# The expert stage of a gated cross-attention and mixture-of-experts block turned round: weights stationary, each expert's tokens as one moving pass of 336 slots

## What is computed

```python
x = x + tanh(g_xattn) * attention(layernorm(x), ctx)     # 120 context rows a sequence, softmax, one head of 256
x = x + tanh(g_ffn)   * experts(layernorm(x))

# experts: H = 256, I = 704, E = 8; every token goes to one expert
e = argmax(router_w @ h)                                 # top 1 of 8
y = down_w[e] @ (silu(gate_w[e] @ h) * (up_w[e] @ h))
```

## Time and profile before

| what | value |
|---|---|
| median of 3 runs (lowest, highest) | 221.98 us (221.41, 222.62) |
| span of the profiled execution | 218.9 us |
| TensorE, matmul busy | 199.7 us, 91% |
| TensorE, weight load busy | 170.9 us, 78% |
| GpSimd (POOL) busy | 136.1 us, 62% |
| VectorE (DVE) busy | 130.8 us, 60% |
| ScalarE (ACT) busy | 109.8 us, 50% |
| HBM read, written | 24.85 MB, 4.72 MB; 135 GB/s over the span |

### The profile page before, as it was taken

How to read it: one execution, slowest core, us unless ns; L and a number is a source line. 1 busy time by engine, 2 the same in 40 slices (tenths; PEclk the granted TensorE clock), 3 DMA queues, 4 the chain that set the end, 5 groups by cost and what they waited for, 6 DMA issues and landing times.

```text
span 218.9 us, 4538 instructions
## 1 busy us (share of the span) xinstructions
PE 199.7 (91%) x1200; PEld 170.9 (78%) x1200; DVE 130.8 (60%) x430; ACT 109.8 (50%) x223; POOL 136.1 (62%) x138
## 2 busy tenths in 40 slices
PE   7899999997665789999999999999999999999960
PEld 3667998985564678888888888888888888888850
DVE  2886899867699125537555537564636565645650
ACT  1478777664500534495269485369475444422410
POOL 3004099495473897339966998987998985212111
PEclk9999999999787589999999999999999999999996
DMA  6999315928600319621581085194003012011000
GB/s 208 340 394 378 135 49 163 368 73 291 217 0 0 99 25 358 211 68 38 189 313 32 0 311 189 34 383 126 1 8 92 0 51 68 9 49 51 5 28 20
DMA packets 11845, 29.43 MB, mean 134 GB/s; under 512 B 1986, under 2 KB 8517, under 8 KB 10790
## 3 DMA queue, kind: packets, MB, share of 16 engines
q1 hardware_dynamic: 6320, 20.20, 25.9%
q0 software_dynamic: 2064, 5.12, 7.8%
q10 hardware_dynamic: 3430, 3.74, 5.1%
HBM read 24.85 MB, written 4.72 MB: 135 GB/s over the span
## 4 chain that ended last, share of the span: by engine, by line
PE 83%; DVE 6%; ACT 3%; DMA 3%; issue 2%; ACTq 1%; POOL 0%; POOLq 0%; DVEq 0%
PE ps L929 36%; PE ps L941 12%; PE ps L908 6%; PE ps L944 5%; PE ps L790 3%; PE ps L729 3%; PE ps L770 3%; DMA both<-in_ctxT 3%; PE ps L811 3%; PE ps L759 2%; PE ps L901 2%; PE ps L800 2%; PE ps L750 2%; PE ps L878 1%; DVE V L1193 1%
## 5 line engine op out<-in xcount | busy, mean ns | idle before, releaser
L929 PE MATMUL ps<-wgu,xhT 128*128 x360 | 83.1, 384 | 1.2 <-DVE xhT L1229 1.2
L929 PEld LDWEIGHTS ps<-wgu,xhT 128*128 128x128 f32 x360 | 66.3, 191 | 12.5 <-issue 1.6
L464 POOL DMA_INDIRECT xin<-x_rows,table x23 | 22.7, 986 | 29.4 <-DVE xin L1264 21.5
L941 PE MATMUL ps<-wd,hT 128*128 x114 | 40.5, 392 | 0.0
L396 POOL TENSOR_TENSOR wgu<-raw_gu,wgu (+1 forms) x12 | 38.6, 3253 | 0.1
L1246 DVE TENSOR_TENSOR A<-xin,ps 128x512 f32<-128x512 f32 (+1 forms) x40 | 20.6, 520 | 25.4 <-ACT xin L656 14.6
L656 ACT ACTIVATE xin<-ps 128x512 f32<-128x512 f32 (+1 forms) x40 | 18.6, 465 | 31.5 <-PE ps L929 31.1
L469 POOL DMA_INDIRECT out<-xin,table x20 | 20.3, 1015 | 18.3 <-DVE xin L1264 13.2
L650 ACT ACTIVATE hT<-ps 128x512 fp32r<-128x512 f32 x20 | 11.8, 592 | 32.9 <-PE ps L908 32.9
L944 PE MATMUL ps<-wd,hT 128*128 x95 | 26.6, 280 | 0.0
L941 PEld LDWEIGHTS ps<-wd,hT 128*128 128x128 f32 x114 | 21.3, 187 | 3.9
(11 more groups left out here) (163 smaller groups left out, 310.7 us busy)
## 6 DMA issues: line engine op xcount, KB each, us to landing
raw_gu<-in_Wgu SPq DMA_DIRECT2D x8, 1408.0 KB, 6.5
both<-in_Wd SPq DMA_DIRECT2D x8, 640.0 KB, 4.3
x_rows<-x ACTq DMA_DIRECT2D x8, 256.0 KB, 3.4
xin<-in_x SPq DMA_DIRECT2D x7, 256.0 KB, 8.8
both<-in_WdL SPq DMA_DIRECT2D x16, 64.0 KB, 4.7
both<-in_ctxT ACTq DMA_DIRECT2D x2, 480.0 KB, 7.1
xin<-x_rows,table POOLq DMA_INDIRECT x23, 3.6
out<-xin,table POOLq DMA_INDIRECT x20, 2.7
```

The costliest lines, as they stand in the source:

```text
L464: pool.indirect_dma_start(out=xg[:, j % SEATS, :], out_offset=None, in_=rows, in_offset=bass.IndirectOffsetOnAxis(ap=table[:, j:j + 1], ax ...
L929: last = pe.matmul(ps[:, g, 0:2 * WIDE if g < 2 else 4 * REST], xhT[:, j % 2, x_part, c, :], w, start=(c == 0 and (x_part, w_part) == (0, 0)),
L941: last = pe.matmul(ps[:, 6, 0:2 * H], hT[:, 0, c, :], wd[:, slot, c].rearrange("p o a n -> p (o a n)"), start=(c == 0), stop=(c == CI - 1) ...
```

## The change

The operands of the expert stage change places. An expert's tokens sit in 336 fixed slots (G = 336: blocks of 128, 128 and 80), so nothing is padded to tiles and no expert's offset is added: slot = rank + 2048 x expert. In up(j) a 128 x 128 piece of the weights is stationary and the 336 tokens stream past. The result has the hidden channels on the partitions, which is what down(j) needs, so turn_h is gone. The 704 channels go in six chunks: first a chunk of 64 gate and 64 up channels side by side (6 matmuls), then five of 128 (12 matmuls each, gate and up in two banks). hm is in SBUF, and both hT parts are made from it there. down(j) has 17 matmuls of 256 columns for each of the three blocks. All of it is unrolled for 8 experts, with fixed addresses. A branch at the end (surplus) makes further passes for an expert with more than 336 tokens; the counts above need none.

The core of the diff:

```diff
-NT = (N + E - 1 + E * (P - 1)) // P
+G = 336
+BL = (G + P - 1) // P
+BLOCK = tuple(min(P, G - P * k) for k in range(BL))
+ORDER = (CI - 1,) + tuple(range(CI - 1))
...
+            for j in range(AHEAD):
+                gather(j)
+            low_gu(SPLIT - 1, 1)
+            low_d(SPLIT - 1, 1)
+            for j in range(E):
+                if j + AHEAD < E:
+                    gather(j + AHEAD)
+                if SPLIT <= j + AHEAD < E:
+                    low_gu(j + AHEAD, 1)
+                    low_d(j + AHEAD, 1)
+                scatter(j)
...
-            def turn_h(j):
-                after(pe, "pe", v_h, 2 * (j + 1))
-                after(pe, "pe", v_hT, j)
-                for c in range(CI):
-                    last = pe.transpose(ps[:, 4 + c // 4, P * (c % 4):P * (c % 4) + P], hm[:, P * c:P * c + P], ident[:])
-                last.then_inc(t_th, 1)
...
+            def product(j, i, kind, bank):
+
                 for c in range(C):
+                    for w_part, x_part in PASSES:
+                        last = pe.matmul(ps[:, bank, 0:G], weights(j, w_part, c, i, kind), xhT[:, j % 2, x_part, c, :],
...
+                for s in range(CI):
+                    q = CI * j + s
+                    i = chunk(q)
+                    if q >= 2:
+                        pe.wait_ge(v_h, q - 1)
+                    if i < CI - 1:
+                        product(j, i, 0, gate_bank(q)).then_inc(t_gu, 1)
+                        product(j, i, 1, up_bank(q)).then_inc(t_gu, 1)
...
+                for k in range(BL):
+                    for s in range(CI - 1):
+                        if k == 0:
+                            pe.wait_ge(v_hT, CI * j + s + 1)
+                        add(k, s)
+                pe.wait_ge(v_hT, CI * j + CI)
+                for k in range(BL):
+                    add(k, CI - 1).then_inc(t_y, 1)
...
-            link(dve.tensor_tensor(offs, ends, padded, ALU.subtract))
...
+            def low_h(q):
+                i = chunk(q)
+                dve.wait_ge(a_hT, q + 1)
+                if i < CI - 1:
+                    dve.tensor_tensor(hT[:, 2 * i + 1, :], hm[:, q % 3, :], hT[:, 2 * i, :].bitcast(F32), ALU.subtract).then_inc(v_hT, 1)
...
+            def experts(j):
+                for s in range(CI):
+                    gated(CI * j + s)
+                    if s:
+                        low_h(CI * j + s - 1)
+                low_h(CI * j + CI - 1)
+                if j + 1 < E:
+                    turned_x(j + 1)
+                finish(j)
```

More of the change, by code:

```diff
@@ L699, in _ @@
             turned_x(0)
-            gathered(1)
-            def drain(j):
-                turned_h(j)
-                for r in range(RING):
-                    act.wait_ge(d_scat[r], 16 * len(range(r, j + 1, RING)))
-            every_tile(act, "act", tile, drain)
+            for j in range(E):
+                experts(j)
+                if SPLIT <= j + AHEAD < E:
+                    split(j + AHEAD)
+            for r in range(SEATS):
+                act.wait_ge(d_scat[r], 16 * BL * len(range(r, E, SEATS)))
@@ L710, in _, with run @@
+            def run(j):
+                if j == E:
+                    act.wait_ge(v_where, 2)
+                for k in range(BL):
+                    gathered(j, k)
+                turned_x(j)
+                split(j)
+                experts(j)
+                act.wait_ge(d_scat[j % SEATS], 16 * BL * (j // SEATS + 1))
+            surplus(act, "act", run)
         @block.tensor
@@ new lines, in _, with run @@
+            turn_x(0)
+            for j in range(E):
+                up(j)
+                if j + 1 < E:
+                    turn_x(j + 1)
+                down(j)
+            def run(j):
+                if j == E:
+                    pe.wait_ge(v_more, 1)
+                    for t in range(NTOK):
+                        last = pe.matmul(ps[:, 2, 0:2 * NX], ohlo_x[:, t, :], uv_x[:, t].rearrange("p a n -> p (a n)"),
+                                         start=(t == 0), stop=(t == NTOK - 1))
+                    for t in range(NTOK):
+                        last = pe.matmul(ps[:, 3, 0:6 * NX], ohlo_x[:, t, :], rsel_x[:, t].rearrange("p a n -> p (a n)"),
+                                         start=(t == 0), stop=(t == NTOK - 1))
+                    last.then_inc(t_more, 1)
+                    pe.wait_ge(v_where, 2)
+                turn_x(j)
+                up(j)
+                down(j)
@@ L1295, with run @@
+            def run(j):
+                if j == E:
+                    where()
+                turned_x(j)
+                experts(j)
+            surplus(dve, "dve", run)
 def kernel(x, ctx_1024, g_xattn, g_ffn, L0_xattn_Wq, L0_xattn_bq, L0_xattn_Wk, L0_xattn_bk, L0_xattn_Wv,
```

755 lines of the change are left out of this document (354 added, 401 removed).

## The result

The changed kernel takes 252.27 us (median of 4 runs, 249.82 to 254.76), the kernel before 221.69 beside it: ratio 1.1306, 95% interval 1.1194 to 1.1419. By the medians it is slower by 30.6 us. The forecast was 226.0 us: it had the direction and missed the size by 26 us. In a later session the same pair had a ratio of 1.1228 (1.112 to 1.1336). The profiled execution of the changed kernel is the slowest of its four, in a state with a lower granted clock (0.901 on average, the others 0.911 to 0.918), which the ratio leaves out. Its parts are therefore compared with a second profile of each kernel too.

What follows compares the result with a forecast made beforehand. TensorE was taken to bound the kernel. First up at 75.9, stage 136.0 and tail 8.5 gave 220.4 us; 2.5 of new wait made 222.9 of span, and 3.1 outside it 226.0 us, ratio 1.018; range 219.5 to 232.

Steps and rivals of the forecast that it cites:

- The matmuls: Expert stage: an up matmul of 336 columns takes 0.153 us, a down matmul of 256 columns 0.12 us.
- the faster rival: TensorE's 15 to 17 ns per matmul over the cycles shrink to 2 ns: 11 us go, time 215; chance 0.13.
- the bare sum: TensorE's up, down and transposing matmuls for 8 experts, without cold start or waits: 134.2 us.
- The new wait: Expert stage: VectorE's low_h held by GpSimd's subtractions, stalling TensorE 0.5 us an expert, 2.5 us in all, bounds 0 and 9.
- The rival of a heavy hold: Each large GpSimd subtraction catches a low_h, some 2.5 us an expert, 15 us with the first, time 239; chance 0.17.
- the cold start: Stage's start: TensorE's clock at the 1.2 GHz level after the wait there, 1.8 us lost, as before.
- The tail: Last matmul to end of span: three residuals and scatters instead of one each, 8.5 us, 2.3 more than before.
- The head: Up to the first up: slots known sooner, but three blocks needed; first up at 75.9, 0.9 us later than before.
- the third gather: Head: the first up needs all three blocks; the third gather starts at 70.6 and is there at 73.9.
- Outside the span: The measured median stands 3.1 us above the profiled span, added to the 222.9 us of forecast span.

Runs made afterwards that it cites:

- the control: The changed kernel with only the turned order of PSUM banks and its waits, the product of gate and up kept in SBUF: 261.71 us, ratio 1.172.

## Why the prediction was wrong

**The matmuls: right.** 0.153 and 0.12 us, as worked out; the faster rival, by which the excess per matmul goes away, is refuted by the last expert's 66 matmuls. With the product in PSUM the stage is 140.3 us, of which 134.2 are the bare sum, 1.7 the half clock at its start (3.5 us of it) and 2.8 waits; 1.6 us are not placed.

**The new wait: the step that failed.** The prediction wrote that a hold is "about 0.75 of GpSimd's instruction, and one instruction only", and from it came 2.5 us with a bound of 9. The runs showed 12.4 us of waits in six experts (the prediction counted five, without the first), and both halves of the step were wrong.

*The length.* A held low_h gets going when GpSimd's instruction ends, not at three quarters of it: 128.13 + 3.69 less its own 0.50 is 131.32, and L454 ends at 131.45. The row behind the step shows the same when read so. L1021 began its real work at about 29.3 and GpSimd's piece ended at 28.59 + 0.98 = 29.57. The 0.25 us between them was a quarter of a piece of 0.98 us by accident; it stays some 0.1 to 0.25 us for one of 3.5.

*One instruction only.* In three of the six experts the hold went on over two boundaries, 5.66 us at expert 3, and over eight or nine, 8.94 us, in the run with pieces. In the three others it was one instruction at a time, as predicted. The row behind the step was of this second kind. L1021 got in between two pieces of a run that began at 27.70, behind 5.40 us of idle time of GpSimd:

```profile
27.70 7.37 POOL L419 TENSOR_TENSOR wgu<-raw_gu,wgu 128x352 fp32r<-128x352 f32 x8 [5.40 <-ACT wgu L574]
```

The prediction took it for all runs.

The size of the holds: the stage without them is 13.7 to 13.8 us shorter, in two runs that remove them in different ways, and the control excludes the banks. The rival of a heavy hold (15 us, 0.17) was the true one, in size and in the main in mechanism. It had three separate catches an expert, and there were one long or two short ones; three subtractions follow each other without a gap in either. The Trainium skill (SBUF — State Buffer, Who interferes with whom) says that the second to issue blocks for the whole instruction. The trace agrees for the single holds (3.69 us beside L454's 3.49) and disagrees for the long ones, which span several instructions; in both it is nearer to the page than to three quarters.

**The clock: counted once.** The prediction had the cold start and no other. In the profiled execution three stalls inside the stage, of 2.2, 3.2 and 3.2 us, each had 3.4 us at the 1.2 GHz level behind them; with the start 13.9 us of the stage are at that level, in the run with the product in PSUM 3.5. Half of the 13.9 is lost: 134.2 + 12.4 + 7.0 = 153.6 of the 154.0 us.

**The tail: a term that was missing.** The three residuals and scatters were right: without the further passes the tail is 8.7 us for a forecast of 8.5. What was missing are TensorE's jumps over bodies that are never run, 7 us. The sum costed the code at the end at nothing, without naming it as such.

**The head: half right.** From the ranks' matmul to the table it took 8.1 us (65.86 to 73.95) against 10.1 before (57.94 to 68.06; 10.0 in the second profile, 63.34 to 73.33), a gain of 2.0 for 1.5 worked out. From the table to the first up 9.4 against 6.9: 2.4 lost, as worked out for the third gather. The rest, 2 to 3 us by the like pairs, lies in the attention ahead of both and was not in the sum. What in the new splits or loads makes it is open: the load order and the place of the splits were tried and left it within the spread of the head. And some 5 of the profiled 8.3 us are that spread.

**Outside the span** it is 1.8 us (254.76 less 253.0) instead of 3.1. But the 3.1 set a median against the span of another execution; where both belong to one, the kernel before has 2.2 us (226.11 less 223.9).

## What to carry to other kernels

Before a VectorE instruction gets two SBUF inputs beside a GpSimd queue, count a hold up to the end of GpSimd's whole run of instructions, since half of them lasted that long here, and leave one of the inputs in PSUM. Code that is never run has a price at TensorE's jump, so nest conditionals that skip together and keep them off the path of the engine that ends last. And compare a stretch of the profile with a second profile of the same kernel before explaining it: here some 5 us of an 8.3 us difference came from the execution and not from the change.

## What the hardware showed unexpectedly

- A subtraction of 0.50 us on VectorE with two SBUF inputs took 5.66 us beside three back-to-back GpSimd subtractions, and 8.94 us when the same work was in pieces of some 0.4 to 1.2 us; with one input in PSUM it took 0.500 to 0.502 us, beside the same work.
- In the same kernels, where GpSimd had stood idle before its first subtraction, VectorE got in at a boundary: 1.57 us, then 3.69 us beside the next large one (53 of 54 runs of subtractions fall in line with this). Why is open.
- A taken jump on TensorE cost 3.1 to 3.7 us over a body of some hundreds of instructions (0.37 for one of six in some profiles), 3.45 us over six of them, and 0.2 us over a body of one. On VectorE, GpSimd and ScalarE it was 0.045 to 0.072 us over full and empty bodies alike, on SyncE up to 0.24 us.
- TensorE stood idle for the context's landing at 7 to 10 us. In twelve of the seventeen profiles, one of them of the kernel before, it was 1.2 us or more, and 3.4 or 6.8 us at the 1.2 GHz level began during it or soon after; in five, one of them of the kernel before, it was 0.2 to 1.1 us, and the clock stayed at 1.00.
- Between spins with no wait among them TensorE stood still for 0.3 to 0.5 us, and 1.0 us ahead of a transpose, put down to nothing in the profile. Why is open; the third block's transposes came late by it.
